# A transformer block with attention and a mixture of experts: another order of the tail's tiles, and the work around it moved between engines and stages

## The reference

```
mod = silu(c) @ wmod                       # scales and shifts per batch: sa ca ga sb cb gb
h = layernorm(x)*(1+ca)+sa ;  x = x + ga * token_statistics_attention(h)
h = layernorm(x)*(1+cb)+sb                 # X below
nx = rmsnorm(X) ; Q = 4 heads of 64 ; K, V: one head of 64, shared by the heads
X  = X + softmax(Q K^T / 8) V @ Wo^T       # 2048 x 2048 scores per head and batch
nx = rmsnorm(X) ; router logits = nx @ Wr^T + bias ; top 2 of 8 experts, gates = softmax of the two
X  = X + shared_swiglu(nx) + sum of gate * expert_swiglu(nx)
out = x + gb * X
```

## Time and profile before

| | us |
|---|---|
| median of 3 runs (1437.9 to 1440.39) | 1438.3 |
| the profiled execution's own time | 1434.95 |
| its span, first to last instruction | 1433.1 |
| TensorE busy in the span | 1262.7 |
| mean granted TensorE clock, share of full speed | 0.966 |

### The profile page before, as it was taken

One profiled execution on the slowest core, in us unless ns is written; L12 is line 12 of the kernel. 1 busy time (PEld: TensorE's weight loads), 2 busy tenths in 40 slices (PEclk: granted clock), 3 DMA queues, 4 the chain that ended last, 5 costly groups with the idle time before them and its releaser, 6 DMA issues.

```text
span 1433.1 us, 18784 instructions
## 1 busy us (share of the span) xinstructions
PE 1262.7 (88%) x5896; PEld 901.3 (63%) x5896; DVE 1087.1 (76%) x2316; ACT 910.0 (63%) x1490; POOL 347.4 (24%) x381
## 2 busy tenths in 40 slices
PE   4974869999999999999989999999766997889984
PEld 2433635666766656767656767665445886777773
DVE  4867768988988887889879889889445664447668
ACT  2646766777877667677787767776547664445541
POOL 0166331112111112011112111111650004323246
PEclk9997889999999999999999999999988999999998
DMA  5001045000000000000000010000112334446534
GB/s 199 8 1 59 1 161 191 9 4 5 8 7 6 4 5 8 5 5 8 8 2 8 6 59 4 9 4 27 67 63 79 106 89 141 140 123 193 167 115 147
DMA packets 61377, 80.71 MB, mean 56 GB/s; under 512 B 12002, under 2 KB 51682, under 8 KB 61026
## 3 DMA queue, kind: packets, MB, share of 16 engines
q1 hardware_dynamic: 36384, 46.81, 10.0%
q0 software_dynamic: 10752, 21.18, 5.5%
q10 hardware_dynamic: 14146, 11.52, 2.4%
HBM read 41.79 MB, written 37.62 MB: 55 GB/s over the span
## 4 chain that ended last, share of the span: by engine, by line
PE 63%; DVE 13%; ACT 8%; issue 6%; POOL 5%; DMA 3%; ACTq 1%; another core or an unknown queue 0%; POOLq 0%; SPq 0%; DVEq 0%
PE PS L1823 7%; PE PS L1752 7%; PE PS L1755 7%; PE PS L1769 6%; PE PS L1720 6%; PE PS L1772 6%; PE PS L1770 6%; DVE mx L1162 4%; PE PS L1849 3%; DVE PL L1192 3%; POOL xbuf L1544 2%; PE PS L1706 2%; PE PS L1807 2%; PE PS L1733 1%; POOL y L1556 1%
## 5 line engine op out<-in xcount | busy, mean ns | idle before, releaser
L784 ACT ACTIVATE PT<-PS 128x1024 f32<-128x1024 f32 x256 | 262.5, 1025 | 193.8 <-PE PS L1755 189.8
L1162 DVE TENSOR_REDUCE mx<-PS 128x1 f32<-128x512 f32 x512 | 344.3, 684 | 41.9 <-PE PS L1720 40.5
L1192 DVE TENSOR_TENSOR PL<-PT,PH 128x512 fp32r<-128x512 f32 x512 | 360.1, 710 | 16.2 <-ACT PH L787 15.5
L787 ACT ACTIVATE PH<-PT 128x1024 fp32r<-128x1024 f32 x256 | 271.5, 1061 | 8.1
L1769 PE MATMUL PS<-PH,VH 128*65 128x512 f32 x512 | 213.6, 417 | 2.1 <-ACT OZ L796 2.1
L1772 PE MATMUL PS<-PL,VH 128*65 128x512 f32 x512 | 203.0, 396 | 9.2 <-DVE PL L1192 9.2
L1770 PE MATMUL PS<-PH,VL 128*65 128x512 f32 x512 | 202.1, 395 | 0.0
L1720 PE MATMUL PS<-KA,Q 128*128 128x512 f32 x384 | 153.9, 411 | 11.3 <-DVE mx L1162 7.3
L1752 PE MATMUL PS<-Q,KA 128*128 128x512 f32 x384 | 130.2, 421 | 2.9 <-DMA Q<-mT 2.9
L1755 PE MATMUL PS<-Q,KB 65*128 65x512 f32 x384 | 122.1, 399 | 0.0
L1772 PEld LDWEIGHTS PS<-PL,VH 128*65 128x65 f32 x512 | 69.6, 136 | 61.0 <-DVE PL L1192 12.4
(11 more groups left out here) (244 smaller groups left out, 2494.0 us busy)
## 6 DMA issues: line engine op xcount, KB each, us to landing
xbuf<-xT SPq DMA_DIRECT2D x26, 384.0 KB, 4.4
xg<-xbuf SPq DMA_DIRECT2D x78, 128.0 KB
ybuf<-yo ACTq DMA_DIRECT2D x78, 128.0 KB
nxT<-in_wexp SPq DMA_DIRECT2D x9, 768.0 KB, 4.2
x<-in_x SPq DMA_DIRECT2D x8, 512.0 KB, 12.0
x_scratch<-x SPq DMA_DIRECT2D x2, 2048.0 KB, 7.3
Z<-z_scratch POOLq DMA_DIRECT2D x32, 128.0 KB, 3.1
nxT<-x_scratch SPq DMA_DIRECT2D x32, 128.0 KB
```

The source lines that it names most:

```text
L784: act.activation(PT[:, gs % 4, :], PS[:, bk:bk + 2, :].rearrange("p a n -> p (a n)"), ACT.Exp, scale=0.125).then_inc(sem("pt"), 1)
L787: act.activation(PH[:, gs % 4, :], PT[:, gs % 4, :], ACT.Copy).then_inc(sem("pt_h"), 1)
L1162: dve.tensor_reduce(mx[:, qb % 2, i, c:c + 1], PS[:, k, :], AX, ALU.max).then_inc(sem("dve_out"), 1)
L1192: dve.tensor_tensor(PL[:, gs % 4, cols], PT[:, gs % 4, cols], phf[:, gs % 4, cols], ALU.subtract).then_inc(sem("pl"), 1)
```

## The change

- **Order of the tail's tiles.** Batch 2's 16 shared tiles come first, then the routed tiles of batch 1 and batch 2, and batch 1's shared tiles last.
- **Last head.** The row sums of its last two blocks no longer go through DRAM. `proj_even` multiplies the even head's half of O alone; `proj_last` multiplies OZ, 65 rows with the sums in the last, by a 65 x 257 matrix whose last column hands the sum through, and DVE divides and adds. For tiles 8 to 11 this is in the loop, for 12 to 15 in the tail. Eight of batch 2's norms move into the head's last quarter (places 74 to 95.5), and the root of the norms is taken in two groups of eight.
- **Batch 1's logits and routing** end in head 7 of 8: the logits that head 6 leaves over at places 4 to 50, the routing at 54 to 92. `rl_scale` is ACT's instead of DVE's, and each normalized tile is kept in DRAM (`nrm`). A scatter now loads its tile from `nrm` by a GpSimd DMA into a ring of four rows; DVE has no part in it. Batch 1's 16 scatters are spread over places 6 to 76 of the last head.
- **Logits of batch 2** use the shared tiles' own transposed parts: four matmuls with 16 columns and two DVE additions in place of a transpose, its copy and two matmuls.
- **Results of routed tiles** are multiplied by gb in DVE's copy from PSUM and stored by SP; the ring has 7 rows instead of 3. ACT has no part in it. Inputs of routed tiles are fetched five steps before their transposes, a ring of six.
- **Sums.** GpSimd forms X2*gb + x for four tiles at once, 128 x 1024 elements an operation: eight for batch 1 from step 20, eight for batch 2 from step 50, the sums of x loaded into two buffers by GpSimd's queue. `combine` is then two DVE operations a tile. For batch 1's shared tiles, last in the tail, gb is multiplied into the shared expert's third matrix before (`rescale`).
- The low part of each expert's third matrix is made by GpSimd (`split_down`) instead of DVE, and splitting begins at step 0 with 1.55 jobs a step (before: step 4, 2.5).
- Several load semaphores are merged.

```diff
-NSX = 3
+NSX = 4
 NXN = 3
 NTI = 39
 NSTEP = 32
 NGS = 8 * NSTEP
 NG = 4
-NXG = 4
+NXR = 6
+NYO = 7
...
-    return pairs([("choose", b)] * 20, n) + pairs([("count", b)] + [("place", b)] * 24, n)
+
+    choose = [("choose", b)] * 22
+    return (pairs(choose[:3], 3) + pairs(choose[3:16], n) + pairs(choose[16:19], 3) + pairs(choose[19:], 3)
+            + pairs([("count", b)] + [("place", b)] * 24, n))
 
 
 def scatter_jobs(b):
-    return [("scatter", b, i) for i in range(NT)]
+    return staged(NT, ("scatter_load", "rest", "scatter"), b)
+
+
+def total_jobs(b):
+    return [(name, b, g) for g in range(4) for name in ("t_mul", "t_add")]
...
+    projections += spread([("proj_even", i) for i in range(8, NT)], 7 * 96 + 44, 7 * 96 + 76)
+    projections += spread([("proj_last", i) for i in range(8, 12)], 7 * 96 + 82, 8 * 96)
+    projections.sort(key=lambda x: x[0])
-        for block in range(4 * bh - 1, 4 * bh + 3):
+        for block in range(4 * bh - 1, min(4 * bh + 3, 30)):
...
-            todo += [(30, ("load_w", NE)), (30, ("load_w", 0))] + spread(rl[18:42], 4, 92)
+            todo += [(30, ("load_w", NE)), (30, ("load_w", 0))] + spread(rl[18:], 4, 50) + spread(route_jobs(0, 2), 54, 92)
         if bh == 7:
-            todo += spread(rl[42:], 4, 16) + spread(route_jobs(0, 2), 18, 60) + spread(scatter_jobs(0), 60, 92)
-            todo += spread(split_jobs(NE), 4, 40)
+            todo += spread(norm_jobs(1)[:4], 74, 84) + spread(norm_jobs(1)[4:8], 86, 95.5)
+            todo += spread(split_jobs(NE), 4, 30) + spread(scatter_jobs(0), 6, 76)
...
-TILES = ([(None, i) for i in range(NT)] + [(0, i) for i in range(NTI)] + [(1, i) for i in range(NTI)]
-         + [(None, NT + i) for i in range(NT)])
+TILES = ([(None, NT + i) for i in range(NT)] + [(0, i) for i in range(NTI)] + [(1, i) for i in range(NTI)]
+         + [(None, i) for i in range(NT)])
 NTL = len(TILES)
 
 
 def tail_order():
 
-    norm = norm_jobs(1)
-    last = [[x for j, p in enumerate(proj_jobs(3, qb)) for x in (norm[4 * qb - 8 + j], p)] for qb in (2, 3)]
-    side = [(-2, 9, [("z_out", 7, 3)] + last[0]),
-            (0, 1, [("z_inv", 7, 3), ("z_back", 7, 3)]),
-            (3, 9, last[1] + norm[8:]),
-            (4, 2.5, [j for ex in range(NE) for j in split_jobs(ex)]),
-            (5, 2.5, rlog_jobs(1)),
-            (25, 1, route_jobs(1, 5) + scatter_jobs(1)),
+    norm = norm_jobs(1)[8:]
+    side = [(-3, 9, [("norm_root", 1)]),
+            (-2, 9, [("proj_last", 12 + i) for i in range(4)]),
+            (-2, 2, norm + [("norm_root", 2)]),
+            (0, 1, [("rl_mm", 1, i) for i in range(NT)]),
+            (0, 1.55, [j for ex in range(NE) for j in split_jobs(ex)]),
+            (2, 1, [("rescale", 0)]),
+            (10, 1, [("rescale", 1)]),
+            (17, 1, [("rescale", 2), ("rescale", 3)]),
+            (20, 1, total_jobs(0)),
+            (17, 1, route_jobs(1, 6)),
+            (28, 3, scatter_jobs(1)),
+            (50, 1, total_jobs(1)),
             (NT + NTI + 3, 0.5, combine_jobs(0)),
-            (NT + 2 * NTI + 1, 1, combine_jobs(1))]
+            (NT + 2 * NTI + 3, 1, combine_jobs(1))]
...
@@ SyncE @@
+            g, i = TILES[s]
+            m = s - NT
+            experts_free(w)
+            keys_free(w)
+            pe_of(w, ("proj_last", NT - 1, 0))
+            if m >= NXR:
+                w.wait_ge(sem("tx"), s - NXR + 1)
+            if g is None:
+                for k in range(NNX):
+                    w.wait_ge(*kept(token(0, NT - 1 - k)))
+                src = nrm[0, i]
+            else:
+                for r in range(NSX):
+                    w.wait_ge(sem(f"d_sx{r}"), 32 * scattered(g, r))
+                w.wait_ge(sem("d_zero"), 16 * 26)
+                src = xbuf[g][i * P:i * P + P, :]
+            sp.dma_start(xr[m % NXR], src).then_inc(sem(f"d_xr{m % NXR}"), 16)
+
+        def store(s):
             g, i = TILES[s]
             if g is None:
+                if s >= NT:
+                    w.wait_ge(sem("ys"), nth[s] + 1)
+                    sp.dma_start(tokens(out, 0)[:, i, :], X2[:, i, :]).then_inc(sem("d_out"), 16)
                 return
-            q = s % NXG
-            experts_free(w)
-            if s >= NXG:
-                w.wait_ge(sem("tx"), s - NXG + 1)
-            for r in range(NSX):
-                w.wait_ge(sem(f"d_sx{r}"), 32 * scattered(g, r))
-            w.wait_ge(sem("d_zero"), 16 * 26)
-            sp.dma_start(xg[:, q, :], xbuf[g][i * P:i * P + P, :]).then_inc(sem(f"d_xg{q}"), 16)
-
-        def gather(n):
-            b, i, s = n // NT, n % NT, n % NG
-            experts_free(w)
-            for r in range(NSX):
-                w.wait_ge(sem(f"d_sx{r}"), 32 * scattered(1, r))
-            if n >= NG:
-                added(w, n - NG)
-            w.wait_ge(sem(f"d_spill{b}"), 16)
-            sp.dma_start(xo[:, s, :], tokens(x1d, b)[:, i, :]).then_inc(sem(f"d_xo{s}"), 16)
+            r = nth[s] % NYO
+            w.wait_ge(sem("yo"), nth[s] + 1)
+            sp.dma_start(ybuf[g][i * P:i * P + P, :], yr[r]).then_inc(sem(f"d_y{r}"), 16)
...
@@ ScalarE, o_out @@
             w.wait_ge(sem("av"), 2 * gs + 2)
-            if block:
+            if block == 31:
+                pe_of(w, ("proj_last", 11, 0))
+            elif block:
...
@@ ScalarE @@
+        def rl_scale(b, i):
+            n = token(b, i)
+            w.wait_ge(sem("rs"), 1 if b == 0 else 2 if i < 8 else 3)
+            nx_free(w, n)
+            if b:
+                experts_free(w)
+            act.activation(nx1[nx_slot(n)] if b else nx[:, nx_slot(n), :], X2[:, b * NT + i, :], ACT.Copy,
+                           scale=rs2[:, b * NT + i:b * NT + i + 1]).then_inc(sem("nx"), 1)
+            if b:
+                w.wait_ge(sem("nx"), n + 1)
...
@@ VectorE @@
+        def proj_last(i):
+            n, k = NT + i, banks.bank["proj_last", i, 0]
+            pe_of(w, ("proj_last", i, 0))
+            pe_of(w, ("max_turn", 7, 2, 0))
+            mark(dve.reciprocal(m16[:, 0, i % 4:i % 4 + 1], PS[:, k, 256:257]))
+            w.wait_ge(own, made[0])
+            out_of(w, ("proj_even", i, 0))
+            dve.scalar_tensor_tensor(X2[:, n, :], PS[:, k, 0:256], m16[:, 0, i % 4:i % 4 + 1], X2[:, n, :], ALU.mult,
+                                     ALU.add).then_inc(sem("dve_out"), 1)
...
@@ VectorE, down @@
+            k, r = nth[s], nth[s] % NYO
+            if k >= NYO:
+                w.wait_ge(sem(f"d_y{r}"), 16 * (k // NYO))
+            if r >= 3:
+                w.wait_ge(sem("w_up"), 2 * (NE + 1))
+                w.wait_ge(sem("w_down"), NE + 1)
+            w.wait_ge(sem("d_late"), 32)
+            dve.tensor_tensor(yr[r], PS[:, 5 + s % 2, 0:256], gbt[:, g, :], ALU.mult).then_inc(sem("yo"), 1)
...
@@ VectorE @@
         def finish(n):
             b, i, s = n // NT, n % NT, n % NG
             w.wait_ge(sem(f"d_pair{s}"), 32 * (n // NG + 1))
             w.wait_ge(sem("gate"), b + 1)
-            w.wait_ge(sem("ys"), shared_done(n))
+            w.wait_ge(sem("t_x2"), 2 * (n // 4 + 1))
             mark(dve.scalar_tensor_tensor(X2[:, n, :], y12[:, s, 0, :], gate[:, b, 0, i:i + 1], X2[:, n, :], ALU.mult, ALU.add))
             w.wait_ge(own, made[0])
             dve.scalar_tensor_tensor(X2[:, n, :], y12[:, s, 1, :], gate[:, b, 1, i:i + 1], X2[:, n, :], ALU.mult,
                                      ALU.add).then_inc(sem("comb"), 1)
-            w.wait_ge(sem("comb"), n + 1)
-            w.wait_ge(sem("d_gbl"), 16)
-            dve.tensor_tensor(X2[:, n, :], X2[:, n, :], gbt[:, b, :], ALU.mult).then_inc(sem("gated"), 1)
-            if not added_by_pool(n):
-                w.wait_ge(sem("gated"), n + 1)
-                w.wait_ge(sem(f"d_xo{s}"), 16 * (n // NG + 1))
-                dve.tensor_tensor(X2[:, n, :], X2[:, n, :], xo[:, s, :], ALU.add).then_inc(sem("add_v"), 1)
 
         dve.memset(eps[:, 0:1], EPS_LN)
         dve.memset(eps[:, 1:2], EPS_RMS).then_inc(sem("eps"), 1)
...
@@ GpSimd @@
+        def rl_scale(b, i):
+            n = token(b, i)
+            w.wait_ge(sem("nx"), n + 1)
+            pool.dma_start(nrm[b, i], nx[:, nx_slot(n), :]).then_inc(kept(n)[0], 16)
+        def scatter_load(b, i):
+            n, r = b * NT + i, (b * NT + i) % NSX
+            pe_of(w, ("q_mm", 1, 1, 3, 0))
+            w.wait_ge(*kept(token(b, i)))
+            if n >= NSX:
+                w.wait_ge(sem(f"d_sx{r}"), 32 * (n // NSX))
+            pool.dma_start(sx[:, r, :], nrm[b, i]).then_inc(sem(f"d_sl{r}"), 16)
...
+        def t_load(k):
+            b, g = divmod(k, 4)
+            w.wait_ge(sem("w_up"), 2 * (NE + 1))
+            w.wait_ge(sem("w_down"), NE + 1)
+            w.wait_ge(sem(f"d_spill{b}"), 16)
+            if k >= 2:
+                w.wait_ge(sem("t_x2"), 2 * (k - 1))
+            pool.dma_start(xo[k % 2], tokens(x1d, b)[:, 4 * g:4 * g + 4, :]).then_inc(sem(f"d_xo{k % 2}"), 16)
+        def t_mul(b, g):
+            ts = slice(b * NT + 4 * g, b * NT + 4 * g + 4)
```

(28 more changed lines are left out.)

351 lines of the change are left out of this document (200 added, 151 removed), and 2 rows, old and new, of the table READERS.

## The result

The changed kernel took 1418.0 us (median of four runs, 1413.5 to 1419.5) against 1439.1 for the kernel before on the same chip: ratio 0.9844, 95% interval [0.9824, 0.9865]. Forecast were 1385 and the range 1358 to 1415. The profiled run took 1413.46 with a span of 1410.5, before 1434.95 and 1433.1. The difference between the two ratios is a part of the answer.

The account below looks back on a forecast made before the run. It took TensorE to bound the kernel, with 63% of the chain of waits. The terms -9.7 - 8 + 0 - 6.4 - 25.5 - 4 gave -53.6 us: 1381.4 as a profiled run, 1385 as a median, range 1358 to 1415.

Parts of the forecast that it names:

- Step 1: Last block of the loop: -9.7 us from 33.2, as the scatters' DVE scalings and waits go; ACT then has most, 23.5.
- step 2: From the last exponential to the tail's first transposes: -8 us from 16.0, as the wait for GpSimd goes.
- Step 3: Batch 1's logits and routing a head earlier: 0, the routing costing the same in head 7; bounds -4 and +6.
- Step 4: Opening of the tail, tile 0 to 18: 70.4 to 64 us, -6.4, ACT the longest engine.
- Rival C: Weights in the tail: ACT waits in `split_up` for each expert, +12 us, 1397; chance 12%.
- rival E: Better: GpSimd's sums cost VectorE nothing and the tail's opening is TensorE-bound, -16 us, 1369; chance 14%.
- Step 5: Tail, tile 18 to 109: 278.3 to 252.8 us, -25.5, including routing +5.5, combining +3.5 and GpSimd's sums +9.
- The lock: Tail routing: VectorE operations with two SBUF inputs and GpSimd's sums reading SBUF exclude each other, +9 us.
- rival A: Tail: GpSimd's 24 us of sums hold VectorE for their whole length, TensorE gets no tiles: +15 us, 1400; chance 15%.
- Rival B: Tail: 0.5 us a tile over 2.54 stays, from the ACT, VectorE, TensorE hand-over: 14.5 us over, 1400; chance 10%.
- D: Both scatter phases: GpSimd's load, landing, scatter, landing run serially, +71 us, 1456; decides from about 5.7 us a tile; chance 4%.
- Step 6: End, from tile 109's transposes: 24.9 to 21 us, -4, as GpSimd's addition and two VectorE operations go.

Follow-up runs that it names:

- the second trace: The changed kernel run and profiled again without an edit, on the fourth chip: 1398.4 us against 1412.8 for the kernel before, ratio 0.9902.
- the placing of before: Changed kernel with batch 1's logits and routing back at their old positions, into head 8, scatters behind them at 60 to 95: ratio 0.9781 to the kernel before.
- the version without overlap: Changed kernel with batch 1's sums moved to steps 45 to 52, batch 2's following, batch 1's combining later: ratio 0.9825 to the kernel before.

## Why the prediction was wrong, step by step

The direction was right and the saving two fifths of what was forecast: -21 instead of -53. The steps that failed are 3, 5 and 6, and 3 and 5 carry it.

*Step 1, last block, and step 2.* Right on the waits that go; what bounds the block then was wrong, to the good. It is TensorE's, 19.9 to 20.9 us; I had taken ACT's 23.5, though ACT is busy only 17.3, with norms in its gaps. Step 2 came out 1.6 short.

*Step 3, logits and routing a head earlier: 0 forecast, +15.6 measured.* This step failed first. It charged head 7 with 2.3 us for the routing's block and set against it what head 8 loses. Measured, the routing costs 4.7 more in head 7 than in head 8, the dense logits 2.7. The bound of +6 that the step named, VectorE saturated there, was the case: VectorE is busy 28.8 of 29.1 us. What the step left out is what else stands there: most of the third pair's sixteen projections have their places in head 7, and almost none in the first half of head 8. The clock falls behind the thin block (0.94 in the first block of head 8, 0.98 in the second trace), and that belongs to the 4.7: with the routing in head 8 it is 1.00 throughout. The low clock of head 8's second block (0.94 and 0.89) doesn't; with the scatters late it is 1.00 there, so it comes with the next term. Two more terms had no line in the sum at all. The scatters over the whole head cost 4.9: step 1 had asked whether GpSimd has time enough and found its projections covered, but not that VectorE's reciprocal waits in order for a transfer behind them. And the projections of the last tokens, moved out of the tail as half-depth matmuls, cost head 8 some 4 us: with the placing of before its first three blocks and head 7 take 182.7 us, in the kernel before 178.4, and TensorE spends 4.9 us on fourteen of their sixteen matmuls in the second and third block of the changed kernel. They were not tried by themselves, so this last share is argued. The four make 16.6; 1.1 of that lies in the last block.

*Step 4.* 2.3 better than forecast: I had charged ACT's 3.2 a step, and from tile 8 on it is TensorE's 3.00. The thin cover of the weights held. Rival C falls. Of rival E the better opening came, the free lock didn't.

*Step 5, tile 18 to 109: 252.8 forecast, 266.7 measured.* The other failure. 231.1 are 91 tiles at 2.54. The routing's own part was 5.6 by the tiles of the version without overlap (forecast 5.5). The lock was 13.4 instead of 9: six operations were held for 1.7 to 2.9 us, one for each of the last six of GpSimd's eight, where I had allowed for up to two, the low part of a weight (L1428) was caught as well, and tile 22's xl stood behind four of them. That lies between my price and rival A's. Combining and the 0.04 a tile, 7.2 together, cost nothing. The stops, forecast at 0, were 16.7. I had read five of the kernel before's as VectorE's wait for the ring, which the change removes. That reading was wrong: the scalings don't wait, ACT does, for a late count of TensorE's, and only on the chips with stops; there the changed kernel stops as well, at other tiles. On a chip without them the two kernels differ by 3.1 us in this step. Rival B falls: away from routing and stops the tile runs at 2.54. So does D: a scatter in the tail takes GpSimd 3.1 us, as forecast (and by D's own sums its turning point was 5.8, not 5.7).

*Step 6.* -4 forecast, nothing measured. The term that failed is the last gather's place: forecast 9.6 to 13 us behind tile 109's transposes, measured 17.1 and 16.7. The bound is GpSimd's 32 gathers at 1.25 us with the gaps before them (8.3 and 3.8 us in the first trace, behind combining that waits for the stopped tiles); on the chip without stops the end is 24.9 before and 24.7 after. With combining one step earlier it is 21.4, but tile 97 pays 3.0 for it.

The sum of the failures is 15.6 in step 3, 13.9 in step 5 and 4.3 in step 6, less 2.6 and 2.3 gained in steps 1 and 4, plus 1.6 in step 2: 30.5 of the 32 between -53.6 and -21.5; the rest lies ahead of head 7 and outside the span.

## What to carry to other kernels

Before work is moved to a "neutral" earlier place, list what every engine already has in that place, and every wait in order on an engine whose input comes through the queue that is now fuller. A stop that has no reason in the program (a releaser "remote" or "issue") should be looked for on a second chip before it is put down to the program, and the first engine that stands looked up, not the last. And work on GpSimd is free beside VectorE's operations on PSUM, dear beside those with two SBUF inputs.

## What the runs showed of the hardware

The same kernel differs by 22 to 26 us between chips (before: 1438.7 and 1439.1 where there are stops, 1412.8 to 1416.7 on three without). In the traces it is the tail with its indirect transfers: tiles 18 to 109 took 278.3 and 252.8, and the rest was 6.7 longer in the faster one. Beside eight gathers in a row ACT stands for 4.4 us on the one kind and not on the other; spaced out, the gathers leave no stop there. In such a stop the record of TensorE's semaphore comes 3 to 4 us behind the matmul's own (1254.85 against 1250.7, 1205.97 against 1202.6), and the traces with stops hold 2072 and 2592 fewer records of semaphores than those of the same kernel without. A GpSimd operation over 128x1024 takes 2.4 us (four times the columns of the earlier trace rows for 3.2 times its time), and four of 128x256 without a wait between them can hold a VectorE operation for 3.56 us.
